# Relu of layer two written back to its PSUM pair in a three-layer graph network kernel

## The reference

```python
def _sage_conv(x, src, dst, W_l, b_l, W_r):
    msgs = x[src]
    agg = jax.ops.segment_sum(msgs, dst, num_segments=N_NODES)
    deg = jax.ops.segment_sum(jnp.ones((src.shape[0],), x.dtype), dst, num_segments=N_NODES)
    mean = agg / jnp.maximum(deg, 1.0)[:, None]
    return mean @ W_l + b_l + x @ W_r
h = jax.nn.relu(_sage_conv(x, src, dst, W1_l, b1, W1_r))
h = jax.nn.relu(_sage_conv(h, src, dst, W2_l, b2, W2_r))
...
x = _layernorm(x + (h @ W3 + b3))
```

## Time and profile before

| | |
|---|---|
| runs | 2992.19, 2999.65, 2999.09 us, median 2999.09 |
| span of the profiled execution | 2989.1 us |
| PE busy | 2869.4 us, 96% |
| DVE busy | 2445.0 us, 82% |
| ACT busy | 1997.4 us, 67% |
| POOL busy | 2151.1 us, 72% |
[...]

### The profile page before, as it was taken

How to read it: one execution, slowest core, us unless ns; L and a number is a source line. 1 busy time by engine, 2 the same in 40 slices (tenths; PEclk the granted TensorE clock), 3 DMA queues, 4 the chain that set the end, 5 groups by cost and what they waited for, 6 DMA issues and landing times. The chain is left out here.

```text
span 2989.1 us, 55620 instructions
## 1 busy us (share of the span) xinstructions
PE 2869.4 (96%) x18457; PEld 2581.4 (86%) x18457; DVE 2445.0 (82%) x4001; ACT 1997.4 (67%) x2992; POOL 2151.1 (72%) x1732
## 2 busy tenths in 40 slices
PE   5999999999999999999999999999999989999996
PEld 4888989898888889898988888898989879888885
DVE  5787887879787878878787878788787879899896
ACT  3676766767676767667676767676676746555554
POOL 5777777777776767667777767677777747777776
PEclk9999999999999999999999999999999999999998
DMA  4444444444444445444444444444444366666663
GB/s 131 151 152 145 162 150 149 154 142 161 152 155 148 153 143 165 149 148 154 143 159 154 155 147 153 145 164 149 148 154 145 130 205 232 235 223 226 238 221 141
DMA packets 253121, 488.25 MB, mean 163 GB/s; under 512 B 37615, under 2 KB 165206, under 8 KB 253090
## 3 DMA queue, kind: packets, MB, share of 16 engines
q1 hardware_dynamic: 202498, 387.58, 38.6%
q0 software_dynamic: 50176, 99.91, 10.3%
q10 hardware_dynamic: 416, 0.40, 0.0%
HBM read 284.67 MB, written 206.22 MB: 164 GB/s over the span
## 5 line engine op out<-in xcount | busy, mean ns | idle before, releaser
L487 ACT ACTIVATE h_full<-pair,bias 128x512 f32<-128x512 f32 x784 | 531.6, 685 | 681.2 <-PE pair L861 666.4
L649 DVE TENSOR_TENSOR h_lo<-h_full,h_hi 128x1024 fp32r<-128x1024 f32 x392 | 651.7, 1663 | 188.3 <-ACT h_hi L489 188.2
L391 POOL TENSOR_TENSOR xb<-xn,b_row 128x1024 f32<-128x1024 f32 x196 | 471.5, 2405 | 297.7 <-DVE y L671 295.9
L345 POOL DMA_INDIRECT xe<-in_x_dram,e_stage x392 | 500.9, 1278 | 176.9 <-issue 97.7
L872 PE MATMUL pair<-w_hi,h_hi 128*128 128x256 f32 x1960 | 565.4, 288 | 26.6 <-DVE h_lo L649 24.5
L872 PE MATMUL pair<-w_lo,h_hi 128*128 128x256 f32 x1960 | 555.3, 283 | 0.0
L872 PE MATMUL pair<-w_hi,h_lo 128*128 128x256 f32 x1960 | 555.2, 283 | 0.0
L489 ACT CAST h_hi<-h_full 128x1024 fp32r<-128x1024 f32 x392 | 412.0, 1051 | 12.5
L872 PEld LDWEIGHTS pair<-w_hi,h_hi 128*128 128x128 f32 x1960 | 375.6, 192 | 51.7 <-DVE h_lo L649 47.7
L500 ACT ACTIVATE o<-y,nb,rs 128x256 f32<-128x256 f32 x784 | 407.2, 592 | 5.6 <-DVE nb L702 5.3
L861 PE MATMUL pair<-xt_hi,w_hi 128*128 128x512 f32 x980 | 401.6, 410 | 7.9 <-DVE xt_lo L645 4.3
(11 more groups left out here) (124 smaller groups left out, 6439.6 us busy)
## 6 DMA issues: line engine op xcount, KB each, us to landing
xn<-in_x_dram SPq DMA_DIRECT2D x196, 512.0 KB, 4.0
out_dram<-o SPq DMA_DIRECT2D x196, 512.0 KB, 2.6
seg<-seg_tab SPq DMA_DIRECT2D x74, 512.0 KB, 5.1
xdb_tab<-xdb SPq DMA_DIRECT2D x49, 512.0 KB, 4.8
h_tab<-src_h SPq DMA_DIRECT2D x49, 512.0 KB
h_tab<-dst_h SPq DMA_DIRECT2D x49, 512.0 KB, 6.3
xn<-h_tab SPq DMA_DIRECT2D x49, 512.0 KB, 5.1
xb<-xdb_tab SPq DMA_DIRECT2D x49, 512.0 KB, 4.1
```

Source lines behind the costliest of these rows:

```text
L345: nc.gpsimd.indirect_dma_start(out=xe[:, kind, s], out_offset=None, in_=x, in_offset=bass.IndirectOffsetOnAxis(ap=e_stage[:, kind, s:s + 1 ...
L391: nc.gpsimd.tensor_tensor(xb[:, b], xn[:, u], b3_row[:, :].unsqueeze(1).to_broadcast([P, S, D]), ALU.add).then_inc(xb_ok, 1)
L487: nc.scalar.activation(h_full[:, n, k], ps[:, k], ACT.Relu, bias=bias[:, n, k:k + 1]).then_inc(hf_ok[n], 1)
L649: nc.vector.tensor_tensor(h_lo[:, h], h_full[:, n], h_hi[:, h].bitcast(f32), ALU.subtract).then_inc(hlo_ok[n], 1)
```

## The change

For `n` = 1 the relu no longer writes `h_full` but the PSUM pair that it reads, in place; the cast and the subtraction read that pair. The wait of the relu for the subtraction of the group before (`hlo_ok[1]`, which kept `h_full[:, 1]` from being overwritten) is dropped for `n` = 1. Layer one (`n` = 0) and the edge stage stay as they are. No instruction is added, removed or moved on any engine; operands change, and one wait goes. Below line 486 the lines of the changed kernel are one higher.

```diff
                 for k in range(K):
                     act.wait_ge(l_ps[n], g * K + k + 1)
-                    after(act, hlo_ok[n], g)
-                    nc.scalar.activation(h_full[:, n, k], ps[:, k], ACT.Relu, bias=bias[:, n, k:k + 1]).then_inc(hf_ok[n], 1)
+                    if n == 0:
+                        after(act, hlo_ok[n], g)
+                    nc.scalar.activation(h_full[:, n, k] if n == 0 else ps[:, k], ps[:, k], ACT.Relu, bias=bias[:, n, k:k + 1]).then_inc(hf_ok[n], 1)
                 act.wait_ge(hf_ok[n], (g + 1) * K)
-                nc.scalar.copy(h_hi[:, h], h_full[:, n]).then_inc(hhi_ok[n], 1)
+                nc.scalar.copy(h_hi[:, h], h_full[:, n] if n == 0 else ps[:, :, :]).then_inc(hhi_ok[n], 1)
...
-            def low_h(g, n, h):
+            def low_h(g, n, h, ps):
                 dve.wait_ge(hhi_ok[n], g + 1)
-                nc.vector.tensor_tensor(h_lo[:, h], h_full[:, n], h_hi[:, h].bitcast(f32), ALU.subtract).then_inc(hlo_ok[n], 1)
+                nc.vector.tensor_tensor(h_lo[:, h], h_full[:, n] if n == 0 else ps[:, :, :], h_hi[:, h].bitcast(f32), ALU.subtract).then_inc(hlo_ok[n], 1)
...
-                    low_h(g, 1, 2)
+                    low_h(g, 1, 2, pair[u])
```

More of the change, by code:

```diff
@@ L658, in _ @@
             dve.wait_ge(cleared, 7)
-            low_h(0, 0, 0)
+            low_h(0, 0, 0, pair[0])
             dve.wait_ge(b_in, 96)
@@ L750, in body @@
                     if not (last and u == 3):
-                        low_h(g + 1, 0, (u + 1) % 2)
+                        low_h(g + 1, 0, (u + 1) % 2, pair[(u + 1) % 4])
                     edges(i, u, pair[(u + 2) % 4])
```

## The result

| | before | after |
|---|---|---|
| runs | 2992.19, 2999.65, 2999.09, 2993.09 us | 2951.44, 2950.44, 2946.30, 2959.28 us |
| median | 2996.09 us | 2950.94 us |
| ratio | | 0.985, 95% interval 0.983 to 0.987 |
| span of the profiled execution | 2989.1 us | 2949.7 us |

The changed kernel is 45 us faster, and the interval of the ratio leaves out 1. The profiled execution of the changed kernel took 2951.44 us, 1.7 us more than its span.

The account below looks back on a forecast made before the run. PE was taken to bound the row stage, waiting on the late subtraction; 0.27 + 0.64 = 0.91 us per pass, times 48, gave 44 us off the 2999.1 us median: 2955 us, with 2945 to 2978 for 8 in 10.

Parts of the forecast that it names:

- What bounds it: Row stage: PE sets the time; its weight loads waited 47.7 us for h_lo in 97 waits, two per pass.
- low reading of 24.5 us: Row stage: the matmul rows' own waits for h_lo, 24.5 us in 49, kept as the lower estimate of the gain.
- Why the subtraction is late: DVE's two-SBUF-input subtraction stands until GpSimd's addition beside it ends: mean 1663 ns against 1226, 171 us over the program.
- Subtraction from PSUM: Layer-two subtraction on DVE: with pair and h_hi as inputs it takes 1.21 us, without the stall behind GpSimd.
- Steps 0 and 1: PE's third-layer weight loads in the pass's first two steps: gains of 0.27 and 0.64 us, 0.91 us per pass.
- the price of the two waits: PE's loss to late weight loads in steps 0 and 1: 0.27 + 0.71 = 0.98 us per pass, 47 us.
- the residue of 0.07 us in step 1: Wait of PE's weight load left in step 1, as DVE's queue gains only 0.32 us: 0.07 us.
- Relu, cast, dropped wait: Layer-two work on ACT: relu to PSUM at 685 ns, cast 45 ns less, one wait gone; nothing in the sum.
- the rival of a slower in-place relu: ACT's relu into the bank it reads: at three times 685 ns the kernel is 52 us slower, 3051; chance 0.05.
- The time: Whole kernel: 44 us gained, span 2945 us, run time 2955 us.
- 10.0 us "around the span": Whole kernel: median time taken to lie around a profiled span, 10.0 us, added to the 2945 us span to give 2955.
- The low end of the main case: Whole kernel: smallest gain, 40 us, in the main case of 40 to 47 us gained, which had chance 0.63.

Follow-up runs that it names:

- sub_only: Kernel before, with only the layer-two subtraction reading the PSUM pair; relu, cast and wait stay as before: 2951.91 us, ratio 0.985 to the kernel before.
- act_only: Kernel before, with layer-two relu and cast in PSUM and the wait dropped, the subtraction keeping two SBUF inputs: 2996.04 us, ratio 0.9996 to the kernel before.
- pool_copy: Kernel before, with GpSimd's two additions per group (xb, xdb) replaced by plain copies in all but 8 columns: 2960.66 us, ratio 0.9852 to the kernel before.
- pool_memset: Kernel before, with GpSimd's additions into xb and xdb replaced by memsets in all but 8 columns: 2958.61 us, ratio 0.9846 to the kernel before.
- copy_long: Kernel of act_only, with GpSimd's two additions replaced by one-input copies made long, about 2.4 us per group: 2981.85 us, ratio 0.9933 to the kernel before.
- memset_long: As copy_long, but with long GpSimd memsets, which read no SBUF, in place of the copies: 2959.13 us, ratio 0.9851 to the kernel before.
- the repetition: The changed kernel run again without any edit: 2948.36 us, ratio 0.9843 to the kernel before.
- sub_twice: Changed kernel with the layer-two subtraction made twice, the first result going to the unused half of h_full: 3019.65 us, ratio 1.0047 to the kernel before.
- keep_wait: Changed kernel with the layer-two relu's wait for the subtraction of the group before put back: 2948.01 us, ratio 0.9839 to the kernel before.
- edge_stage: Changed kernel with the edge stage's relu, cast and subtraction in PSUM too, PE waiting there for the subtraction: 2930.92 us, ratio 0.9754 to the kernel before.

## Why the prediction was right

*What bounds it.* Right, with one slip. PE was the bound, but of the 47.7 us of weight-load waits 3.5 belong to the end of the row stage and stayed; 44.2 could be had, and the row stage gave 44.2. The low reading of 24.5 us, the matmul rows, would have been wrong by almost half. In step 0 of the pass of the earlier trace rows, where the weight load waited 0.23 us, the rows of the matmuls, with their modelled tails (0.40 us, the next one after 0.23), leave no gap:

```profile
1494.61 0.40 PE L861 MATMUL pair<-xt_lo,w_hi 128*128 128x512 f32 x1
1494.84 1.04 PE L851 MATMUL pair<-ident,xe 128*128 128x128 f32 x8
1495.87 0.39 PE L872 MATMUL pair<-w_hi,h_hi 128*128 128x256 f32 x1
```

*Why the subtraction is late.* Right, and shown from both sides: the operand alone brings it (sub_only, 0.985), the rest without it doesn't (act_only, 0.9996), and taking away what it stands beside brings it too (pool_copy 0.9852, pool_memset 0.9846). copy_long against memset_long adds that it matters whether GpSimd reads SBUF: with long copies the two-input subtraction had a mean of 1668 ns, with long memsets 1209.

*Subtraction from PSUM.* Taken at 1.21 us, measured 1208 ns, and the freedom from the stall, for which there was no row before, is there in all 144 that start beside an addition: none takes over 1.23 us. Reading PSUM had no price: 1208 ns with it, 1225 without.

*Steps 0 and 1.* 0.91 us per pass predicted, 0.92 measured. That the two are so close is partly luck, since two terms were too large by about the same amount.

The first is the price of the two waits, 0.98 us per pass, or 47 us, which seemed confirmed by the 47.7 us of the view. That view holds the 3.5 us of the row stage's end, so the two don't confirm each other: the 96 waits that went are 44.2 us, 0.92 per pass, and the idle times in the earlier trace rows, 0.23 and 0.68 us, say 0.91. The 0.98, taken from the distances between loads, supposes that all later loads come sooner by the whole of a wait. They don't quite: from the load behind the transposes of step 0 to the transposes of step 1 it was 1504.98 - 1495.87 = 9.11 us and is 1477.57 - 1468.41 = 9.16.

The second is the residue of 0.07 us in step 1. In the profiled execution of the changed kernel it is nothing; there PE comes those 0.05 us later, and the subtraction took 1.19 and not 1.21 us. In the repetition PE's stretch is as before (1476.98 - 1467.86 = 9.12 us) and a residue of about 0.05 us is there; its gain is 2318.5 - 2273.0 = 45.5 us, 0.95 per pass. What makes that stretch 9.12 us in one execution and 9.16 in the other no run here shows. That step 1 is at the edge of costing was right: sub_twice put 1.17 us back in one wait per pass.

*Relu, cast, dropped wait.* Priced at nothing, measured at nothing (act_only 0.9996, keep_wait within 0.4 us). The relu to PSUM took 662 ns, near the low bound; the rival of a slower in-place relu fell with it.

*The time.* 2955 predicted, 2950.9 measured. The 10.0 us "around the span" was misnamed: what lies around a span is 1.7 us, and the other 8.3 are by how much the profiled execution was faster than the median of the runs. As a bridge from that span to the median the 10.0 did its work, but the two sums in the prediction are one and the same (the median less 44), not two that agree. The median of before came down to 2996.1 with one more run, and 2996.1 - 44 = 2952, about 1 us from the measured median. That is closer than the runs allow to tell: those of the changed kernel lie from 2946.3 to 2959.3. The low end of the main case, 40 us gained, is worked out from no row, and no run shows a term behind it; the waits that went were 44.2 us.

*What the prediction missed.* It said of DVE's shorter busy time that it isn't the gain, and had nothing on the other direction of the same conflict: that VectorE instructions with two SBUF inputs held GpSimd, its copies (1.84 us for 0.82 in copy_long) and its DMA issues (1.37 us beside a subtraction, where the median is 1.02). POOL is busy 102.5 us less after the change with the same instructions. The small copy behind the addition of step 1 shows it, before and after:

```profile
1505.49 1.19 POOL L342 COPY e_stage<-idx 128x4 int32 x1
```

```profile
1477.98 0.19 POOL L342 COPY e_stage<-idx 128x4 int32 x1
```

In the row stage that is free (POOL waits 356.7 us for `y`), in the edge stage GpSimd is the bound (550 of 589.5 us).

## What to carry to other kernels

Where the mean of a group is above what most of its executions take (here 1663 ns against 1226), put its timeline beside GpSimd's: in these runs the VectorE subtraction with two SBUF inputs and a GpSimd addition or copy took turns, and the one that came second was late (the subtraction 2.58 or 1.80 us for 1.23, a copy 1.84 for 0.82). Moving one of the two inputs to PSUM freed it (none of 144 over 1.23 us), and cost PE nothing, since the pair's next writer waits for the subtraction anyhow (PE's weight loads waited 3.5 us for it, 47.7 before); the price in VectorE time was nothing (1208 ns against 1225). Count the gain by the weight loads' waits of the bounding engine and not by the stall (171 us of stalls were 44 us of time), leave out waits that lie elsewhere, and ask for each stage anew who sets it: in the second stage the same edit paid because GpSimd did (its issues 24.4 us less, the span 20.7).

## What the runs showed of the hardware

- A VectorE subtraction with two SBUF inputs and GpSimd's additions and copies, which read SBUF, held each other in both directions. In the kernel before 148 subtractions start beside an addition and end 1.08 to 1.10 us after it, though one takes 1.22 alone, so by my estimate some 0.14 us (1.22 - 1.08) pass beforehand. A GpSimd copy that came second took 1.84 us for 0.82, a small one 1.19 for 0.19.
- Which comes next when several GpSimd instructions follow each other is not settled. In copy_long the subtraction of 1501.51 stood through two copies and went ahead of a third; in the kernel before one that started at 64.21, beside a DMA issue, stood through the addition that began 0.37 us after it and took 3.87 us.
- A memset of GpSimd, which writes SBUF and reads none, didn't hold it (1209 ns in memset_long).
- GpSimd's DMA issues beside such VectorE instructions were longer too: a mean of 1126 and 1108 ns in the changed kernel against 1076 and 1033 in edge_stage, with one such instruction fewer per step. In the changed kernel's edge stage the issues beside none took at most 1.03 us, the others up to 2.09.
- An in-place relu on a PSUM bank was no slower than one to SBUF: 662 against 686 ns in the changed kernel.
